# Six fill matmuls of TensorE moved from ahead of the first outputs to behind two waits, and two dropped

## The reference

```python
A = jnp.einsum('bhncd,bhned->bhnce', kbc, kc)
T = jnp.linalg.inv(eye + jnp.tril(A, -1))
u = T @ vc
w = T @ kbc
def body(S, inp):
    q_i, k_i, u_i, w_i = inp
    attn = jnp.where(tri, jnp.einsum('bhcd,bhed->bhce', q_i, k_i), 0.0)
    u_i = u_i - w_i @ S
    o_i = q_i @ S + attn @ u_i
    S = S + jnp.einsum('bhcd,bhce->bhde', k_i, u_i)
    return (S, o_i)
S, o = jax.lax.scan(body, S0, (mv(qc), mv(kc), mv(u), mv(w)))
```

## Time and profile before

| | |
|---|---|
| time, median of 3 runs | 579.94 us (578.74 to 581.18) |
| profiled execution, its own time | 578.74 us |
| its span, first to last instruction | 577.0 us |
| TensorE busy (matmuls) | 544.8 us, 94% |
| weight loads | 368.4 us, 64% |
| VectorE, ScalarE, GpSimd busy | 393.0, 325.4, 176.4 us |
| mean granted clock of TensorE | 0.99 of full speed |
| chain of waits, share of TensorE | 83% |

### The profile page before, as it was taken

One profiled execution on the slowest core, in us unless ns is written; L12 is line 12 of the kernel. 1 busy time (PEld: TensorE's weight loads), 2 busy tenths in 40 slices (PEclk: granted clock), 3 DMA queues, 4 the chain that ended last, 5 costly groups with the idle time before them and its releaser, 6 DMA issues.

```text
span 577.0 us, 17529 instructions
## 1 busy us (share of the span) xinstructions
PE 544.8 (94%) x7487; PEld 368.4 (64%) x7487; DVE 393.0 (68%) x766; ACT 325.4 (56%) x575; POOL 176.4 (31%) x343
## 2 busy tenths in 40 slices
PE   3799999999999999999999999999999999989995
PEld 2445555555555556777877778768555777667774
DVE  5697999999999964335264444455799951478775
ACT  2317788888878887555655563666850540135441
POOL 7100111354455442001010100638999009010202
PEclk9799999999999999999999999999999999999998
DMA  4878856553532000001000000011384310000001
GB/s 123 164 216 207 210 133 149 123 127 79 93 58 58 5 4 2 0 0 39 1 0 2 1 1 0 1 39 39 60 129 87 85 23 3 6 2 1 0 20 55
DMA packets 54163, 33.82 MB, mean 59 GB/s; under 512 B 38965, under 2 KB 45621, under 8 KB 54086
## 3 DMA queue, kind: packets, MB, share of 16 engines
q1 hardware_dynamic: 48870, 31.65, 24.5%
q10 hardware_dynamic: 5216, 1.05, 1.0%
HBM read 20.83 MB, written 9.44 MB: 52 GB/s over the span
## 4 chain that ended last, share of the span: by engine, by line
PE 83%; DVE 6%; ACT 4%; DMA 3%; issue 2%; SPq 1%; POOL 0%; POOLq 0%; DVEq 0%; ACTq 0%
PE ps L1841 11%; PE ps L1826 10%; PE ps L1588 7%; PE ps L1589 7%; PE ps L1590 7%; PE ps L1916 6%; PE ps L2030 4%; PE ps L2163 3%; PE ps L1805 3%; PE ps L2164 3%; DMA qst<-shift_sb 2%; PE ps L2022 2%; ACT prob L704 2%; PE ps L1678 2%; PE ps L1680 2%; PE ps L1679 2%
## 5 line engine op out<-in xcount | busy, mean ns | idle before, releaser
L1243 DVE TENSOR_REDUCE nmx<-ps 128x1 f32<-128x1024 f32 x128 | 154.1, 1218 | 14.8 <-PE ps L1806 13.4
L704 ACT ACTIVATE prob<-ps 128x512 f32<-128x512 f32 x256 | 137.4, 597 | 26.4 <-PE ps L1826 25.9
L1841 PE MATMUL ps<-prob,vp 128*32 128x128 f32 x2048 | 78.9, 278 | 0.0
L1826 PE MATMUL ps<-qst,kst 50*128 50x512 f32 x256 | 73.5, 491 | 4.4 <-ACT prob L704 3.6
L1841 PEld LDWEIGHTS ps<-prob,vp 128*32 128x32 f32 x2048 | 49.1, 109 | 39.9 <-ACT prob L704 22.4
L1115 DVE TENSOR_TENSOR h_lo<-hf,h_hi 128x512 fp32r<-128x512 f32 x48 | 33.1, 689 | 52.4 <-ACT h_hi L608 50.2
L1588 PE MATMUL ps<-h_hi,w_lo 128*128 128x512 f32 x144 | 58.2, 404 | 2.4 <-DVE h_lo L1115 2.4
L1589 PE MATMUL ps<-h_lo,w_hi 128*128 128x512 f32 x144 | 56.9, 395 | 0.0
L1590 PE MATMUL ps<-h_hi,w_hi 128*128 128x512 f32 x144 | 56.7, 394 | 0.0
L1805 PE MATMUL ps<-kst,qst 48*128 48x512 f32 x128 | 52.6, 412 | 0.6 <-DVE nmx L1243 0.5
L1806 PE MATMUL ps<-kst,qst 48*128 48x512 f32 x128 | 51.5, 404 | 0.0
(11 more groups left out here) (262 smaller groups left out, 1086.8 us busy)
## 6 DMA issues: line engine op xcount, KB each, us to landing
qst<-q_scratch SPq DMA_DIRECT2D x31, 192.0 KB, 4.4
kst<-k_scratch SPq DMA_DIRECT2D x31, 192.0 KB, 4.8
w_raw<-L_ffn_h_w SPq DMA_DIRECT2D x8, 256.0 KB, 3.7
kd<-ka SPq DMA_DIRECT2D x8, 256.0 KB, 6.3
X<-L_attn_x SPq DMA_DIRECT2D x4, 256.0 KB, 5.4
qst<-shift_sb SPq DMA_DIRECT2D x64, 4.0 KB
q_scratch<-w_hi SPq DMA_DIRECT2D x2, 512.0 KB, 5.1
k_scratch<-w_lo SPq DMA_DIRECT2D x2, 512.0 KB, 3.3
```

Source lines behind the costliest of these rows:

```text
L704: nc.scalar.activation(prob[:, n % PROBS, GT * (t % 2):GT * (t % 2) + GT], ps[:, RINGB + i % RING, :], ACT.Exp, scale=SCORE_SCALE).then_in ...
L1243: nc.vector.tensor_reduce(nmx[:, u % 2, j:j + 1], pair, AX.X, ALU.max, negate=True).then_inc(max_done, 1)
L1826: nc.tensor.matmul(ps[:, RINGB + i % RING, :], kst[r:r + 50, p, P * t:P * t + P], half_of(qst[r:r + 50, p, :], u % 2), start=True, stop=Tr ...
L1841: last = nc.tensor.matmul(ps[32 * j:32 * j + 32, PVB, P * half:P * half + P], vp[:, h, t, :], prob[:, n % PROBS, c:c + P], start=(t == 0), ...
```

## The change

One call of keep_busy is taken out, and another has another count. The six fill matmuls that stood between inputs_of_state(0) and begin_outputs(0, 0) go; behind the waits for m_ready and g_ready there are now six instead of two. They write bank 0, as the two did; the six that go wrote bank 4.

```diff
@@ -2037,12 +2037,11 @@
             transition_products(0)
             keep_busy(7, 5)
             inputs_of_state(0)
-            keep_busy(4, 6)
             for n in range(4):
                 begin_outputs(0, n)
             pe.wait_ge(m_ready, 1)
             pe.wait_ge(g_ready, 1)
-            keep_busy(0, 2)
+            keep_busy(0, 6)
             times_inverse(1)
             transition_products(1)
             pe.wait_ge(b_ready, 4)
```

## The result

The changed kernel took 584.74 us (median of 20 runs, 580.91 to 593.62), the kernel before, run beside it, 580.98 us (20 runs). The ratio is 1.0069 with a 95% interval of 1.0041 to 1.0098, or +4.0 us. The forecast was +2.25 us on 579.94, 582.2 us, with a range up to 584.0: the right sign, and too small. The same kernel was measured twice more, in later batches: 1.0028 (0.9994 to 1.0062) and 1.0022 (0.9999 to 1.0045), +1.6 and +1.3 us. That the three differ is part of the result.

What follows compares the result with a forecast made beforehand. TensorE's queue was taken to bound the kernel up to the state loop. Queue +0.75 us plus low clock 1.5 us gave +2.25 us on the median 579.94, so 582.2 us, range 579.2 to 584.0.

Steps and rivals of the forecast that it cites:

- The block of 256: TensorE's holds are ends of blocks of 256 instructions; the one in begin_outputs moves from after the fourth pair to the tenth.
- The rival in which nothing holds TensorE longer: The hold moves along at 0.67 us or is no fetch; net two fill matmuls fewer, -0.66 us, 579.3 us; chance 0.14.
- The hold's length, 2.18 us: In begin_outputs TensorE reaches the block's end at 459.90 and waits until 462.08 us, 2.18 us instead of 0.67.
- The queue's +0.75 us: TensorE's queue from begin_outputs to the state loop, without the clock: +0.75 us, bounds +0.6 and +1.0.
- gives nothing back: The second and third hold exist before, so instruction supply sets the pace there and late slack is nil.
- The clock's fall: After the longer hold, from near 462 us, the granted clock drops from 1.00 to 0.50 in most executions.
- Its price, 1.5 us: Cost of a 3.4 us low-clock stretch, half the length seen, behind the hold: 1.5 us, ends 0 to 3.4.
- low twice as long: Clock at 0.50 for about 6.8 us in times_inverse(1) and transition_products(1): price 3.4, total +4.15 us, 584.1 us; chance 0.14.
- The shift that reaches the end in full: The state loop starts when TensorE gets to it, so any shift of TensorE's queue moves the kernel's end equally.

Runs made afterwards that it cites:

- e5: Kernel before plus twelve short matmuls (24 instructions) at 448 us, ahead of the four fill matmuls there; +2.7 us, interval 1.0003 to 1.0090.
- e7: Changed kernel plus 52 short matmuls (104 instructions) at 448 us; +0.4 us on the kernel before, interval 0.9987 to 1.0028.
- e1: Kernel before with only the six fill matmuls ahead of begin_outputs removed, the two behind the waits kept; +1.2 us, interval 1.0000 to 1.0040.
- e3: Kernel before with the six fill matmuls ahead of begin_outputs cut from 512 columns to 16; +1.5 us, interval 1.0008 to 1.0043.
- e4: Kernel before without the two fill matmuls behind the waits, the six ahead of begin_outputs kept; +0.1 us, interval 0.9984 to 1.0019.
- three and three: Kernel before with three fill matmuls ahead of begin_outputs instead of six and three behind the waits instead of two, run twice; +0.3 us both times.
- g2: Kernel before plus 10 short identity products (40 instructions) at TensorE's start; +1.6 us, interval 1.0009 to 1.0048.
- g3: Changed kernel plus 26 short identity products (104 instructions) at TensorE's start; +0.9 us on the kernel before, interval 1.0001 to 1.0030.
- g1: Kernel before plus 46 short identity products (184 instructions) at TensorE's start; -0.9 us, interval 0.9967 to 1.0003.
- e6: First run of the kernel before with three fill matmuls ahead of begin_outputs and three behind the waits; +0.3 us, interval 0.9971 to 1.0038.
- e2b: Second run of the kernel before with six fill matmuls instead of two behind the waits, the six ahead kept; -1.2 us, interval 0.9951 to 1.0009.
- g4: Changed kernel plus 46 short identity products (184 instructions) at TensorE's start; +1.0 us on the kernel before, interval 0.9993 to 1.0041.

## Why the prediction was right or wrong

**The block of 256: right.** Begin_outputs started at once, the hold came at the tenth pair, TensorE waited for about as long as it had been let run ahead. e5 and e7 show the count, e1 that the removed fill is the half that does it. The rival in which nothing holds TensorE longer gave e1 a stretch of 14.8 us; it was 18.2. That was the rule of the Trainium skill ("Runtime: NRT & Kernel Launch", Instruction fetch mechanics), that the cost of crossing a block is mostly hidden. The traces agree at some ends of blocks, as at the one that e5 moved into the fill, where the kernel before has no hold, and not at others, with holds of 0.2 to 2.3 us.

**The hold's length, 2.18 us: high.** It was 1.85, 1.64, 1.54 and, in e1, 1.59. The step took 462.08 us, the moment at which the block came in the one trace of before, as fixed. From the start of inputs_of_state(0) that is 3.91 us; in the traces above it was 3.66, 3.45, 3.35 and 3.41. One trace gave one draw of a delay that scatters by half a microsecond and more.

**The queue's +0.75 us: wrong.** The third trace has -0.1. Two parts failed: the block came 0.56 us sooner (3.35 against 3.91), and "gives nothing back" was false, since the second and third hold shrank: in the earlier trace rows they take 0.25 and 0.47 us, in the first trace of after 0 and 0.28, with transition_products(1) in 1.96 us as one piece.

**The clock's fall: right in kind, and the largest term.** I gave its being seen 0.56 in all. It fell in two of three traces of the changed kernel and in e1's.

**Its price, 1.5 us: too small, and this is the step that failed the number.** The estimate was made for 3.4 us at the low clock. e3, where it was 3.4 us, cost 1.4: the rate was right. But the fall lasted 6.8 us in both traces of the changed kernel that have it and in e1's, behind holds of 1.59 to 1.85 us in begin_outputs. (The hold's length alone doesn't set it: e5's 2.32 us, in inputs_of_state(0), was followed by 3.4 us.) Its terms in the first trace are (0.40 + 2.33) - (0.23 + 1.94) = +0.56 us of outputs, 2.86 - 1.60 = +1.26 of fill and 5.13 - 3.88 = +1.25 of times_inverse(1): 3.1 us. The earlier trace rows had shown this length, 6.8 us at 0.50 behind a sparse stretch. I halved it with no row that said so, since TensorE would be busier; it was busy for 6.80 of 6.80 us. The forecast's third rival, "low twice as long", had the mechanism, at a chance of 0.14. That its +4.15 us lies within 0.2 us of the first batch's +4.0 is in part luck: at the changed place the trace has +2.84, 3.1 from the clock and -0.2 from the queue, and the rest of the +4.0 lies elsewhere.

**The shift that reaches the end in full: not shown.** The whole time follows the stretch of the one trace only loosely. e4's stretch is 1.0 us longer with a whole of +0.1, those of three and three are 0.7 and 0.5 us shorter with +0.3 twice, and inputs_of_state(0) itself starts anywhere from 458.0 to 460.6 us in unchanged code.

**What of +4.0 us was not in the sum.** In the first batch the runs stood 17.4 us at the low clock, where the kernel before stood 8.7 to 10.0 in the other batches (its own in that batch were not at hand). The second and third batch have +4.0 and +2.0. The three ratios follow these numbers, and the first trace's rate, 3.1 us for 6.8, makes of a surplus of about 8 us an estimate of 3.7. The single runs say the same: of those that the ratios count, 16 of 19, 6 of 8 and 5 of 11 had a mean clock under 0.990 (5 and 3 of 27 for the kernel before in the last two batches), and they took 3.1, 3.5 and 2.0 us more than the others of their batch. Why the clock falls in some executions and batches and not in others, after the same hold, stays open. The third trace had 1.86 us busy in 3.4 and kept it; the first had 1.55, the second 1.76 and e3's 2.48, and they lost it, but such a number depends on where the row's stretch begins. The +4.0 us of the first batch is thus the change at its dearest, not its usual cost; the middle of the three is +1.6 us, nearer to the forecast than the first.

## What to carry to other kernels

Where TensorE runs hundreds of short products, count instructions, not only time: every 256th can be a hold, fill with few instructions per microsecond hides it, and taking such fill out can gain nothing and here cost more than it took. An idle stretch that looks cheap in the chain has a second price in the clock, and its length should be taken from the low stretches that the trace shows, not from a shorter one that no row has. And where a number of the sum rests on one fetch or one transfer of one trace, its scatter belongs in the range.

## What the runs showed of the hardware that I had not expected

- The ends of blocks are so regular that holds can be moved by adding idle instructions ten or four hundred and fifty microseconds upstream (e5, e7, g2, g3), and the whole time moved by 2.5 us of 581 between two such places (g1, g2). How long the hold is at a place was foretold badly.
- The delay of a block scatters from execution to execution: where the hold stands in begin_outputs and nothing was added upstream, it ends 2.88 (e6) to 3.95 us (e4) from the start of inputs_of_state(0), and 4.18 in e2b's. e4 shows 5.1 us from one block to the next (461.96 to 467.06) while the inverse's loads were under way. That those loads slow the fetch was not tried apart.
- A hold of 0.92 us with short fill ahead was followed by a low clock (e3); holds of 1.15 us in times_inverse(1) (e4), 1.16 (g4) and 1.54 us (the third trace of the changed kernel) were not.
- Six matmuls of 16 columns with 128 columns of weights took 0.77 us, 0.13 us each, where six of 512 columns take 1.60 (0.27 each): a thirty-second of the columns takes half of the time.
